# State products, context keys, values and set-up moved ahead at two stage joins of an eight-stage fp32 kernel, with six products of constants added

## The chip, the cores and the metric

The kernel runs on one core of a Trainium2 chip. The metric is the device time of the whole program in microseconds (us). The program is one launch, all data are fp32, and the host only transposes and regroups weights.

## The reference

Two sequences of 1024 rows of 256 columns (x, 2048 rows in all) go through eight residual stages. Each stage computes a layer norm of x, or works on x itself, and adds a gated result to x. They are lettered A to H. Two joins matter here: from E to F, and from F to G.

```python
def step(c, xt):                                   # stage F, a gated recurrence of two steps
    ft = sigmoid(xt @ wf.T + c @ uf.T + bf)
    it = sigmoid(xt @ wi.T + c @ ui.T + bi)
    gt = tanh(xt @ wc.T + c @ uc.T + bc)
    return ft * c + it * gt
h = tanh(x @ wo.T + c_final @ uo.T + bo)
# stage G: attention of 16 heads over 77 context rows, biased and masked
q = (LN(x) @ q_w.T + q_b); k = (ctx @ k_w.T + k_b); v = (ctx @ v_w.T + v_b)
attn = q k^T * scale + bias;  probs = masked softmax(attn)
x = x + tanh(g) * ((probs @ v) @ o_w.T + o_b)
```

In stage F the batch is the time axis: the two sequences are the two steps, and the first step starts from one given state c0, the same for every row. So the products of c0 with uf, ui and uc are constants of the run. In stage G the keys and values depend on the context alone and not on x.

## The kernel before

Each engine has its own instruction list, written out by hand stage after stage, and engines meet at counting semaphores. There is no planner: the order in each list is the order of the calls in the code. TensorE (PE) runs sim_pe (E), rnn_pe (F) and heads16_pe (G) in turn, VectorE (DVE) runs sim_dve, rnn_dve, norm_dve and heads16_dve, and ScalarE (ACT) has functions of the same names. x stays in SBUF as 16 tiles of 128 rows. Each finished tile has its statistics taken by finish (the update of x is L488, the statistics L490), and counts up the semaphore x_new. A matmul of the code is fp32 and appears as two instructions in the trace, so the counts in the rows are twice those of the code.

**Join E to F.** The last products of E are L1109. TensorE waits for all 16 tiles of E (x_new) and then makes the state products: three gates by two by two blocks with one moving column, L1308, into bank 7. VectorE waits for them, makes four small bias operations from them (L1424 to L1427), and only then norm_dve: seven small operations on the statistics (L656 to L662), a square root by ScalarE (L676), a reciprocal (L667). normed(0) then writes the first four normalised tiles (L1436), which TensorE transposes in two groups of two tiles (turn_x, L1323), each copied out by ScalarE (L1390). The gate products follow (from_x, L1330: 12 matmuls, 24 instructions, for each batch), ScalarE squashes them (L1397), and VectorE combines (gated, L1443 to L1452).

**Join F to G.** F has four steps s of two tiles and two batches. The last step ends with outputs(3) on TensorE (L1361 and L1368), summed(3) on VectorE (L1456, then L1459 twice), tanh by ScalarE (L1406) and update(3) on VectorE (L488 and L490 four times). TensorE waits for the last tile (x_new), then makes the context keys (L298, bank 4), the context values (values_ctx, L305, bank 7), turn_x(0) (L315) and queries(0) (L325). VectorE runs norm_dve, normed(0) (L505), then the set-up: four memsets of the value and count buffers and five small operations on the mask and one more memset (L510 to L521), then spread_k(0) (L526). It waits for the queries (take_q, L548), and goes on with spread_k(1), normed(1), shift(0, 0) (L565, L573, L574), spread_k(2), spread_k(3) and spread_v (L537 to L542). scores are L340, transposes of the weights L353, products with the values L367, projections L379.

```python
pe.wait_ge(sem("x_new"), NT + done("E", "x_new"))     # rnn_pe, ahead of the state products
...
dve.wait_ge(sem("F_u0_ps"), 1)                         # rnn_dve, ahead of the four bias operations
...
pe.wait_ge(sem("x_new"), NT + done("F", "x_new"))     # ahead of heads16_pe(pe, "G")
```

PSUM has eight banks. In F, bank 0 takes transposes and the last output products, banks 1 to 6 the gates of both batches, banks 7 and 6 the outputs. "ident" is the 128 x 128 identity, and "slots" a constant table, 512 columns wide; both are in SBUF from the start.

## Time and profile before

| what | value |
|---|---|
| median of 3 runs | 1467.87 us (1462.8, 1467.87, 1468.26) |
| profiled execution, its own time | 1465.94 us |
| its span, first to last instruction | 1464.1 us |
| TensorE busy | 1172.4 us, 80% |
| VectorE busy | 903.3 us, 62% |
| ScalarE busy | 523.9 us, 36% |
| GpSimd busy | 249.9 us, 17% |
| mean granted TensorE clock | 0.895 |

The clock is the share of full speed that TensorE was granted: 1.00 is 2.4 GHz and 0.50 is 1.2 GHz. The busy time of TensorE counts pipelined products from start to modelled end, so it overstates how full the engine is. The time outside the span is 1.84 us. The profiled execution lies between the lowest and the middle of the three runs.

### The profile page before, as it was taken

The numbers are of one execution on the slowest core, as the hardware profiler recorded it, in microseconds if no ns is written. First come the engines' busy times: TensorE is split into PE (matmuls) and PEld (weight loads), VectorE is DVE, ScalarE is ACT, GpSimd is POOL, SyncE is SP. The second block draws the span as 40 slices with busy tenths as digits, with TensorE's granted clock in tenths as the row PEclk, the third lists the DMA queues.
The fourth block names the chain that finished last, engine by engine and source line by source line (L and its number), as shares of the span: only waits on it lengthen the run. The fifth ranks groups of instructions, "written<-read, shape, count | busy, mean of one in ns | idle before, by whom it ended". The sixth has DMA issues, their size and how long they took to land.

```text
span 1464.1 us, 22555 instructions
## 1 busy us (share of the span) xinstructions
PE 1172.4 (80%) x8580; PEld 894.5 (61%) x8580; DVE 903.3 (62%) x2229; ACT 523.9 (36%) x1161; POOL 249.9 (17%) x220
## 2 busy tenths in 40 slices
PE   5988899995998898866999879898788963999500
PEld 4665688884456545653565768787566762888400
DVE  6889832348457646984645545255899975655333
ACT  3543434242347553531424211223244435434100
POOL 0009043300500000002010000000000002655376
PEclk9999989995899999997999879899799985999855
DMA  9200045400000003000000440000021002555443
GB/s 324 100 2 1 11 121 146 138 1 0 1 1 2 1 1 116 1 1 22 1 22 1 120 159 0 0 1 0 35 71 71 36 1 83 165 161 156 107 133 118
DMA packets 60001, 89.01 MB, mean 61 GB/s; under 512 B 21315, under 2 KB 50877, under 8 KB 57085
## 3 DMA queue, kind: packets, MB, share of 16 engines
q1 hardware_dynamic: 52413, 67.18, 14.1%
q0 software_dynamic: 7488, 20.46, 5.4%
q8 instruction: 68, 1.11, 0.3%
q14 instruction: 32, 0.26, 0.1%
HBM read 60.73 MB, written 26.89 MB: 60 GB/s over the span
## 4 chain that ended last, share of the span: by engine, by line
PE 53%; DVE 23%; issue 11%; ACT 6%; POOL 5%; DMA 1%; SPq 0%; POOLq 0%; DVEq 0%; ACTq 0%
PE ps L2454 5%; PE ps L1330 4%; POOL hall L2690 4%; PE ps L773 4%; PE ps L760 4%; PE ps L1836 3%; PE ps L2468 2%; DVE work L583 2%; PE ps L1850 2%; PE ps L367 2%; DVE work L574 2%; DVE work L573 2%; PE ps L1909 2%; PE ps L340 1%; DVE work L565 1%
## 5 line engine op out<-in xcount | busy, mean ns | idle before, releaser
L2679 POOL DMA_INDIRECT hall<-hall_rows,tile_idx x80 | 75.8, 948 | 423.2 <-DVE tile_idx L2597 376.4
L340 PE MATMUL ps<-hall,work 128*128 128x308 f32 x256 | 81.0, 442 | 12.1 <-DVE work L548 4.9
L1771 ACT ACTIVATE work<-ps,work 128x256 f32<-128x256 f32 x128 | 58.8, 472 | 84.7 <-DVE work L1659 84.6
L2454 PE MATMUL ps<-big,work 128*128 x320 | 84.4, 387 | 0.0
L367 PE MATMUL ps<-work,hall 78*32 78x128 f32 (+1 forms) x2048 | 69.7, 277 | 11.6 <-DVE work L584 8.5
L460 ACT COPY work<-ps 78x1024 f32<-78x1024 f32 (+1 forms) x64 | 64.3, 1004 | 40.4 <-PE ps L353 39.3
L367 PEld LDWEIGHTS ps<-work,hall 78*32 78x32 f32 (+1 forms) x2048 | 52.8, 110 | 36.5 <-ACT work L460 22.3
L353 PE MATMUL ps<-pack_const,work 128*78 128x128 f32 (+1 forms) x512 | 70.1, 281 | 3.0 <-issue 3.0
L583 DVE RECIPROCAL work<-ps 128x128 f32<-128x128 f32 x64 | 60.8, 951 | 13.7 <-PE ps L367 13.3
L2690 POOL DMA_INDIRECT hall<-expert_rows,back_idx x64 | 61.7, 964 | 39.4 <-DMA expert_rows<-work 20.2
L2652 DVE SCALAR_TENSOR_TENSOR x<-hall,work,x 128x256 f32<-128x256 f32 x64 | 31.2, 487 | 57.0 <-DMA hall<-expert_rows,back_idx 55.2
L1836 PE MATMUL ps<-big,dpack 128*128 128x384 f32 (+1 forms) x160 | 63.9, 563 | 1.9 <-ACT big L1748 1.0
L1330 PE MATMUL ps<-work,pack_F 128*128 128x256 f32 x288 | 64.8, 385 | 0.7 <-ACT work L1390 0.7
L353 PEld LDWEIGHTS ps<-pack_const,work 128*78 128x78 f32 (+1 forms) x512 | 56.1, 135 | 14.9 <-issue 11.5
L2601 DVE TENSOR_TENSOR work<-work,ps 128x128 f32<-128x128 f32 x80 | 23.2, 290 | 67.4 <-ACT work L2515 67.4
L340 PEld LDWEIGHTS ps<-hall,work 128*128 128x128 f32 x256 | 45.3, 197 | 25.3 <-DVE work L548 5.8
L1330 PEld LDWEIGHTS ps<-work,pack_F 128*128 128x128 f32 x288 | 55.5, 194 | 8.6 <-ACT work L1390 1.1
L760 PE MATMUL ps<-work,big 128*128 128x256 f32 x256 | 59.6, 393 | 0.7 <-ACT work L786 0.7
L2454 PEld LDWEIGHTS ps<-big,work 128*128 128x128 f32 x320 | 55.9, 195 | 4.6
L279 POOL TENSOR_TENSOR hall<-hall,mask_add 128x1232 f32<-128x1232 f32 x16 | 40.9, 2580 | 97.4 <-DMA hall<-in_fside 97.4
L773 PE MATMUL ps<-big,work 128*128 128x256 f32 x256 | 56.6, 379 | 0.0
L760 PEld LDWEIGHTS ps<-work,big 128*128 128x128 f32 x256 | 50.7, 199 | 8.4 <-ACT work L786 1.1
(497 smaller groups left out, 2695.2 us busy)
## 6 DMA issues: line engine op xcount, KB each, us to landing
expert_rows<-work SPq DMA_DIRECT2D x40, 256.0 KB, 2.2
masked_bias<-hall SPq DMA_DIRECT2D x8, 1232.0 KB, 5.2
dpack<-masked_bias SPq DMA_DIRECT2D x8, 1232.0 KB, 5.8
hall<-in_fside SPq DMA_DIRECT2D x8, 616.0 KB, 7.4
dpack<-in_pack_D SPq DMA_DIRECT2D x1, 4115.0 KB, 15.7
hall_rows<-hall SPq DMA_DIRECT2D x2, 2048.0 KB, 10.7
big<-in_w SPq DMA_DIRECT2D x4, 1024.0 KB, 11.1
big<-in_pack_B SPq DMA_DIRECT2D x1, 2052.0 KB, 10.1
```

Source lines behind the costliest of these rows:

```text
L340: mm = nc.tensor.matmul(o, A["qT"][:, c, b * P:(b + 1) * P], KV["kbd"][:, c, b, k * 4 * SC:(k + 1) * 4 * SC], start=True, stop=True)
L353: mm = nc.tensor.transpose(ps[0:SK[L], PT_BANK + h // 4, h % 4 * P:(h % 4 + 1) * P], weights_of(L, u)[:, h, :], ident)
L367: mm = nc.tensor.matmul(ps[j * HB32:(j + 1) * HB32, 4, half:half + P], lhsT, A["pT"][0:SK[L], u % 2, h * P:(h + 1) * P], start=g == 0, sto ...
L460: nc.scalar.copy(A["pT"][0:SK[L], u % 2, :].rearrange("p (k n) -> p k n", k=2), ps[0:SK[L], PT_BANK:PT_BANK + 2, :]).then_inc(s("pT_ready" ...
L583: link(ve.reciprocal(den, DEN_REG))
L760: mm = nc.tensor.matmul(ps[:, 1 + f // 2, f % 2 * D:(f % 2 + 1) * D], w["fc"][:, c * F0 + f * P:c * F0 + (f + 1) * P], BW["xnT"][:, c, :], ...
L773: mm = nc.tensor.matmul(ps[:, 5 + b, 0:D], BW["hT"][:, f, b * P:(b + 1) * P], w["proj"][:, f * D:(f + 1) * D], start=f == 0, stop=f == FC - 1)
L1330: mm = nc.tensor.matmul(ps[:, 1 + 3 * b + g, co * FJ * P:(co + 1) * FJ * P], w[kind + "fic"[g]][:, ci * D + co * P:ci * D + (co + 1) * P], ...
L1836: mm = nc.tensor.matmul(ps[:, bank, 0:n], w["wqkv"][:, ci * 3 * HDH + col:ci * 3 * HDH + col + P], LB["xnT"][:, ci, at:at + n], start=ci = ...
L2454: mm = nc.tensor.matmul(ps[:, GU_B[j % 2], 0:2 * INTER], MW["xT"][:, j % 2, c * P:(c + 1) * P], big[:, bass.ds(at + c * 2 * INTER, 2 * INT ...
L2679: gp.indirect_dma_start(out=FETCH_BUF[:, j % HT, :], out_offset=None, in_=hall_rows[:, :], in_offset=bass.IndirectOffsetOnAxis(ap=tile_idx ...
L2690: gp.indirect_dma_start(out=hall[:, t % NGB * TOP + k, :], out_offset=None, in_=expert_rows[:, :], in_offset=bass.IndirectOffsetOnAxis(ap= ...
```

## The change

What it does, and then the whole diff:

- The state products of F no longer wait for E's last tile. They go to bank 1 and are followed by two products of ident with slots (keep_busy(2, 2), into bank 2, which nobody reads before it is overwritten). VectorE makes its four bias operations after normed(0). TensorE waits for them once, ahead of the first gate product.
- The wait for F's last tile ahead of stage G is gone. The context keys come right behind the last output products. The values wait for the seventh increment of F_ysum_ready, the first L1459 of summed(3), which frees bank 7; four products of ident with slots (keep_busy(4, 5)) follow them, ahead of turn_x(0).
- G's set-up on VectorE becomes a function of its own and is called between gated(3, 1) and summed(3) in rnn_dve. Stage A makes the same set-up where it did. The wait for C_in moves with it.

```diff
--- before.py
+++ after.py
@@ -232,6 +232,11 @@
         block = ctx.enter_context(nc.Block())
 
 
+        def keep_busy(count, bank):
+
+            for _ in range(count):
+                nc.tensor.matmul(ps[:, bank, :], ident, pk["const"]["slots"], start=True, stop=True)
+
         UNITS = [(b, c) for b in range(B) for c in range(DC)]
         NU = len(UNITS)
 
@@ -381,7 +386,9 @@
                 mm.then_inc(s("y_ps"), 1)
 
             if L == "G":
+                pe.wait_ge(sem("F_ysum_ready"), (FS - 1) * FJ + 1)
                 values_ctx()
+                keep_busy(4, 5)
             turn_x(0)
             queries(0)
             if L == "A":
@@ -489,6 +496,22 @@
                                          op0=ALU.mult, op1=ALU.add))
             nc.vector.bn_stats(stats[:, t, :], x[:, t, :]).then_inc(done, 1)
 
+        def heads16_setup_dve(dve, L):
+            link, ve = chain_dve.link, nc.vector
+            link(ve.memset(KV["vpad"][0:SK[L]], 0.0))
+            link(ve.memset(KV["count"][0:SK[L]], 0.0))
+            for g in range(2):
+                link(ve.memset(KV["count"][0:SK[L], :, g, g * HD16:(g + 1) * HD16], 1.0))
+            if L == "G":
+                dve.wait_ge(sem("C_in"), LOADS["C"])
+                link(ve.tensor_copy(keep, mask8[:, :]))
+                link(ve.tensor_scalar(keep, keep, -1.0, 1.0, ALU.mult, ALU.add))
+                all_masked, counted = small[:, 4:4 + B], small[:, 8:8 + B]
+                link(ve.tensor_reduce(all_masked, mask_add[:, :, :], AX.X, ALU.max))
+                link(ve.tensor_scalar(all_masked, all_masked, 0.0, None, ALU.is_lt))
+                link(ve.tensor_tensor(counted[0:SC], keep, all_masked[0:SC], ALU.max))
+            link(ve.memset(small[:, 511:512], 0.0))
+
         def heads16_dve(dve, L):
             link = chain_dve.link
             w = pk[L]
@@ -496,8 +519,6 @@
             ve = nc.vector
             dve.wait_ge(sem("const_in"), 48)
             dve.wait_ge(sem(f"{L}_in"), LOADS[L])
-            if L == "G":
-                dve.wait_ge(sem("C_in"), LOADS["C"])
 
             def normed(n):
                 for b in range(B):
@@ -507,18 +528,8 @@
 
             normed(0)
             hm = pk["const"]["headmask"]
-            link(ve.memset(KV["vpad"][0:SK[L]], 0.0))
-            link(ve.memset(KV["count"][0:SK[L]], 0.0))
-            for g in range(2):
-                link(ve.memset(KV["count"][0:SK[L], :, g, g * HD16:(g + 1) * HD16], 1.0))
-            if L == "G":
-                link(ve.tensor_copy(keep, mask8[:, :]))
-                link(ve.tensor_scalar(keep, keep, -1.0, 1.0, ALU.mult, ALU.add))
-                all_masked, counted = small[:, 4:4 + B], small[:, 8:8 + B]
-                link(ve.tensor_reduce(all_masked, mask_add[:, :, :], AX.X, ALU.max))
-                link(ve.tensor_scalar(all_masked, all_masked, 0.0, None, ALU.is_lt))
-                link(ve.tensor_tensor(counted[0:SC], keep, all_masked[0:SC], ALU.max))
-            link(ve.memset(small[:, 511:512], 0.0))
+            if L == "A":
+                heads16_setup_dve(dve, "A")
             dve.wait_ge(s("kv_ps"), 1 + done(L, "kv_ps"))
 
             def spread_k(u):
@@ -539,7 +550,7 @@
                                               ALU.add))
                     if L == "G":
                         link(ve.tensor_scalar(KV["vpad"][0:SC, b], KV["vpad"][0:SC, b], keep[:, b:b + 1], None, ALU.mult))
-                        link(ve.tensor_scalar(KV["count"][0:SC, b], KV["count"][0:SC, b], counted[0:SC, b:b + 1], None, ALU.mult))
+                        link(ve.tensor_scalar(KV["count"][0:SC, b], KV["count"][0:SC, b], small[0:SC, 8 + b:9 + b], None, ALU.mult))
                 dve.sem_inc(s("kv_ready"), 1)
 
             def take_q(n):
@@ -1295,20 +1306,20 @@
         FS = HT // FJ
         GW = carve([("xn", (FJ, B, D)), ("xnT", (2, DC, B, FJ * P)), ("gate", (B, 3, DC * FJ * P)), ("c1", (DC, FJ * P)), ("c2", (DC, FJ * P)),
                     ("t", (FJ, D)), ("y", (FJ, B, D)), ("bias", (2, 3 * DC)), ("c0", (DC,))])
-        FY_BANK, FU_BANK = (7, 6), 0
+        FY_BANK, FU_BANK, FU0_BANK = (7, 6), 0, 1
 
         def rnn_pe(pe):
             w = pk["F"]
             pe.wait_ge(sem("F_in"), LOADS["F"])
 
-            pe.wait_ge(sem("x_new"), NT + done("E", "x_new"))
             for g in range(3):
                 for co in range(DC):
                     for ci in range(DC):
-                        mm = nc.tensor.matmul(ps[:, 7, g * DC + co:g * DC + co + 1],
+                        mm = nc.tensor.matmul(ps[:, FU0_BANK, g * DC + co:g * DC + co + 1],
                                               w["u" + "fic"[g]][:, ci * D + co * P:ci * D + (co + 1) * P],
                                               w["c0"][:, ci:ci + 1], start=ci == 0, stop=ci == DC - 1)
-            mm.then_inc(sem("F_u0_ps"), 1)
+            mm.then_inc(sem("F_u0"), 1)
+            keep_busy(2, 2)
 
             def turn_x(s):
                 for j in range(FJ):
@@ -1335,6 +1346,8 @@
 
             def from_x(s, b):
                 for g in range(3):
+                    if b == 0 and s == 0 and g == 0:
+                        pe.wait_ge(sem("F_u0"), 2)
                     if b == 0 and s:
                         pe.wait_ge(sem("F_gate_ready"), (s - 1) * 6 + g + 1)
                     if b and s:
@@ -1419,13 +1432,16 @@
             link, ve = chain_dve.link, nc.vector
             w = pk["F"]
             dve.wait_ge(sem("F_in"), LOADS["F"])
-            dve.wait_ge(sem("F_u0_ps"), 1)
-            b0, b1 = GW["bias"][:, 0, :], GW["bias"][:, 1, :]
-            link(ve.tensor_tensor(b0, ps[:, 7, 0:3 * DC], w["bias"], ALU.add))
-            link(ve.tensor_scalar(GW["bias"][:, 0, 0:2 * DC], GW["bias"][:, 0, 0:2 * DC], 0.5, None, ALU.mult))
-            link(ve.tensor_scalar(GW["bias"][:, 1, 0:2 * DC], w["bias"][:, 0:2 * DC], 0.5, None, ALU.mult))
-            link(ve.tensor_copy(GW["bias"][:, 1, 2 * DC:3 * DC], w["bias"][:, 2 * DC:3 * DC]))
             norm_dve(dve, "F")
+
+            def biases():
+                dve.wait_ge(sem("F_u0"), 1)
+                b0, b1 = GW["bias"][:, 0, :], GW["bias"][:, 1, :]
+                link(ve.tensor_tensor(b0, ps[:, FU0_BANK, 0:3 * DC], w["bias"], ALU.add))
+                link(ve.tensor_scalar(b0[:, 0:2 * DC], b0[:, 0:2 * DC], 0.5, None, ALU.mult))
+                link(ve.tensor_scalar(b1[:, 0:2 * DC], w["bias"][:, 0:2 * DC], 0.5, None, ALU.mult))
+                link(ve.tensor_copy(b1[:, 2 * DC:3 * DC], w["bias"][:, 2 * DC:3 * DC]))
+                dve.sem_inc(sem("F_u0"), 1)
 
             def normed(s):
                 if s:
@@ -1467,6 +1483,7 @@
                         finish(s * FJ + j + b * HT, GW["y"][:, j, b, :], None, 6, None, sem("x_new"))
 
             normed(0)
+            biases()
             normed(1)
             for s in range(FS):
                 gated(s, 0)
@@ -1476,6 +1493,7 @@
                         normed(s + 1)
                     update(s - 1)
                 gated(s, 1)
+            heads16_setup_dve(dve, "G")
             summed(FS - 1)
             update(FS - 1)
 
@@ -2798,7 +2816,6 @@
             heavy_pe(pe)
             sim_pe(pe)
             rnn_pe(pe)
-            pe.wait_ge(sem("x_new"), NT + done("F", "x_new"))
             heads16_pe(pe, "G")
             moe_pe(pe)
```

## Rows read from the trace of the kernel before

**Rows 1.** Page, the chain of work that ended last, by engine.

```profile
PE 53%; DVE 23%; issue 11%; ACT 6%; POOL 5%; DMA 1%; SPq 0%; POOLq 0%; DVEq 0%; ACTq 0%
```

**Rows 2.** Timeline, E to F: start, us, engine, line, op, operands, count, [idle before <-releaser].

```profile
913.33 1.03 PE L1109 MATMUL ps<-work,hall 128*128 128x256 f32 x4
...
915.37 0.43 DVE L490 BATCH_NORM_STATS2 stats<-x 128x6 f32<-128x256 f32 x1
...
915.95 4.54 PE L1308 MATMUL ps<-pack_F 128*128 128x1 f32 x24 [1.59 <-DVE stats L490]
...
921.43 0.19 DVE L656 TENSOR_TENSOR small<-stats 128x16 f32<-128x16 f32 x1
...
923.47 1.38 DVE L1436 TENSOR_SCALAR work<-x,mean,rstd 128x256 f32<-128x256 f32 x4
...
925.73 1.11 PE L1323 MATMUL ps<-pack_const,work 128*128 128x128 f32 x4 [0.68 <-ACT work L1390]
...
927.52 12.02 PE L1330 MATMUL ps<-work,pack_F 128*128 128x256 f32 x48 [0.68 <-ACT work L1390]
```

**Rows 3.** Busy time in stretches around E to F; columns: us, PE, PEld, DVE, ACT, POOL, PEclk, DMA.

```profile
916.70:920.50 3.80, 3.79 (x19) 3.70 (x18) 0.00 (x0) 0.00 (x0) 0.00 (x0) 0.50 0.00 0
...
927.50:930.40 2.90, 2.88 (x7) 2.35 (x8) 0.77 (x3) 1.27 (x1) 0.00 (x0) 0.50 0.00 0
930.40:941.00 10.60, 9.93 (x50) 8.56 (x49) 2.36 (x4) 3.10 (x7) 0.00 (x0) 1.00 0.00 0
941.00:1015.70 74.70, 73.29 (x347) 63.95 (x345) 36.27 (x69) 24.22 (x53) 0.00 (x0) 1.00 0.00 1
```

**Rows 4.** Timeline, F to G.

```profile
1016.02 1.99 PE L1368 MATMUL ps<-pack_F,work 128*128 128x256 f32 x8 [0.38 <-DVE work L1452]
1018.05 0.69 DVE L1456 TENSOR_TENSOR work<-ps,rows_F 128x512 f32<-128x512 f32 x1 [2.08 <-PE ps L1368]
1018.78 1.29 DVE L1459 TENSOR_TENSOR work<-ps,work 128x512 f32<-128x512 f32 x2
...
1023.70 2.42 PE L298 MATMUL ps<-ctxT,dpack 128*128 128x154 f32 x8 [5.69 <-DVE stats L490]
...
1025.72 0.73 DVE L505 TENSOR_SCALAR work<-x,mean,rstd 128x256 f32<-128x256 f32 x2
...
1026.61 0.91 DVE L510 MEMSET hall<- 77x1024 f32 x1 [0.16 <-issue]
...
1029.29 0.06 DVE L521 MEMSET small<- 128x1 f32 x1
1029.33 0.62 PE L315 MATMUL ps<-pack_const,work 128*128 128x128 f32 x4
...
1030.63 2.00 PE L325 MATMUL ps<-work,dpack 128*128 128x256 f32 x8 [0.68 <-ACT work L439]
1032.66 1.00 DVE L548 TENSOR_SCALAR work<-ps,dpack 128x256 f32<-128x256 f32 x2 [2.41 <-PE ps L325]
...
1046.76 3.42 PE L325 MATMUL ps<-work,dpack 128*128 128x256 f32 x8
```

**Rows 5.** Busy time in stretches from F into G.

```profile
1018.00:1022.50 4.50, 0.02 (x1) 0.00 (x0) 4.21 (x9) 2.51 (x3) 0.00 (x0) 1.00 0.00 0
...
1023.70:1029.30 5.60, 5.60 (x16) 4.22 (x17) 4.45 (x20) 0.21 (x1) 0.00 (x0) 0.50 0.00 0
...
1049.80:1190.00 140.20, 126.53 (x1557) 98.47 (x1555) 131.80 (x219) 56.95 (x70) 0.00 (x0) 1.00 0.16 56
```

**Rows 6.** Timeline, prices at full clock: one-column, 512-column, transposes, gate products.

```profile
863.35 1.05 PE L1127 MATMUL ps<-work 128*128 128x1 f32 x8 [1.18 <-DVE work L1275]
...
696.64 7.03 PE L2251 MATMUL ps<-dpack,big 128*128 128x512 f32 x16
...
963.14 0.66 PE L1323 MATMUL ps<-pack_const,work 128*128 128x128 f32 x4 [0.68 <-ACT work L1390]
963.63 10.53 PE L1330 MATMUL ps<-work,pack_F 128*128 128x256 f32 x48
```

## The prediction, on record before the changed kernel ran

> **What bounds the kernel now.** I read the page's chain first: TensorE holds 53% of it, VectorE 23% [rows 1]. That is an average over eight stages, so I went to the two joins that the change touches, with the timeline for the order of events and the stretches for what each engine and the granted clock did.
>
> At the join E to F the reader sees a queue of four things, one behind the other. E's last statistics end at 915.80. TensorE then makes 24 one-column products until 920.49, VectorE makes four bias operations, the norm starts at 921.43, and the first tiles are written from 923.47 [rows 2]. Only then come transposes and gate products, from 927.52. Behind them TensorE is busy 73.29 of 74.70 us at clock 1.00 [rows 3]: stage F is bound by TensorE, so what its first gate product gains, its last one gains too.
>
> At the join F to G the last tile releases the keys at 1023.70; keys and values run at clock 0.50, busy 5.60 of 5.60 us [rows 5], and the transposes of G start behind them at 1029.33. The normalised tiles had been ready since 1026.45, so TensorE is late and not VectorE. VectorE then waits 2.41 us for the queries [rows 4]. From there on it has work in a row, and in G's steady part it is busy 131.80 of 140.20 us [rows 5]: what the first queries gain, the end gains.
>
> **The sum for E to F.** The norm no longer stands behind products and biases: it starts 0.04 behind the statistics, at 915.84, not 921.43. That is 5.59 us. The tiles follow, the second at 923.47 + 0.69 - 5.59 = 918.57. What TensorE does until then:
> - State products start when E's products stop issuing, 913.33 + 4 x 0.217 = 914.2 (0.217 from 48 in 10.53, less 0.33 of the last, by 47 [rows 6]). One costs (1.05 - 0.25)/7 = 0.114 us at full clock [rows 6] (0.25 is one product's own length), so 24 cost 2.74, until 916.9.
> - Two constant products are four instructions of 512 columns. One costs (7.03 - 0.59)/15 = 0.43 [rows 6], so 1.7, until 918.65, 0.1 behind the second tile. At full clock they cost nothing, covered by the norm.
> - The bias operations (0.94 with their gaps, 920.49 to 921.43 before) lie behind normed(0), in VectorE's wait for the second transposes; the gate products need them some 2 us later. Nothing for them.
>
> Then the clock. In the trace before, TensorE stops with 256-column products at 914.36, makes one-column ones from 915.95, and the clock is 0.50 from 916.7. It stays there while the engine is busy 3.79 of 3.80 us with them, and comes back at 930.4 after 2.88 us of gate products [rows 3]. If the clock holds after the change, the transposes save 0.45 in the second group (1.11 to 0.66), some 0.2 in the first, and the 48 gate products 12.02 - 10.53 = 1.49 [rows 2, 6]: 5.6 + 2.1 = 7.7 us.
>
> If it falls, TensorE's list itself becomes long. At half clock a one-column product takes about 0.2 (19 of them in 3.80 us [rows 3]) and a constant 0.86 (twice 0.43). With the fall at 916.7 as before, two products are left (0.4) and the constants need up to 3.4, until 920.5, where the tile was ready at 918.6. The constants are wide, though, and 2.88 us of wide products brought the clock back before. I take it that it comes back at their end: transposes at 920.4, then 0.6 + 0.68 + 0.66 + 0.68, gate products at 922.9 and not 927.52, at full clock: 4.6 + 1.5 = 6.1. The bad end is a fall that the constants don't mend, say at 916.2: six products left (1.3), constants 3.4, until 920.9, then 1.1 + 0.68 + 1.1 + 0.68, gate products at 924.4, 3.1 early. I allow them twice the 2.9 us at half clock that they had before, which takes half of 2.9 back: 1.7.
>
> The weight load of a one-column product has a rule against the price I use. The Trainium skill, "TensorE: Matmul & The Clock Gate", section "LDWEIGHTS (loading the stationary operand)", gives columns / 1.2 GHz, 107 ns, whatever the granted clock; by it the six left at the bad end would cost 0.6 and not 1.3, and that end would be 2.4 and not 1.7. The trace disagrees: 0.114 apart at 1.00, 0.2 at 0.50, so 1.7 stands.
>
> **The sum for F to G.** The set-up moves ahead of summed(3). It takes 1029.35 - 1026.61 = 2.74, and VectorE has a wait of 2.08 there from 1015.97 [rows 4]. summed(3) starts at 1018.8 and not 1018.05, and everything behind it, tanh, updates and norm, is 0.8 later: a loss. Queued behind it are TensorE's values (bank 7), ScalarE's tanh and all of F's last updates. In return spread_k(0) follows normed(0) at once, which nobody waited for.
>
> TensorE: keys at 1017.9, 8 x 0.13 (0.217 for 256 columns, scaled to 154), then a wait for the first L1459, 1019.5 + 0.8 = 1020.3; values 8 x 0.217 until 1022.0; four constant products, eight instructions, 3.4, until 1025.4. The tiles of G come at 1026.1 + 0.8 and 1027.3. At full clock all of that is covered, with 1.5 us to spare, and the transposes end at 1027.8 and not 1029.95: 2.2 us. ScalarE's copy and the queries (2.00 [rows 4]) shift with them. But before, the queries already ran at full clock, which 5.6 us of keys and values had brought back; now a pause of 1.5 us, short transposes and a copy stand ahead of them. Should the clock fall there, the queries cost 3.42 (a later group at half clock, [rows 4]) and not 2.00, the transposes 0.4 more: 0.3 left, and the first scores at half clock take that too. Between 2.2 and about -0.3 I take 1.0, near the middle, as nothing in the rows says which.
>
> Sum: 6.1 + 1.0 = 7.1, call it 7.0. The profiled execution took 1465.94 (span 1464.1 and 1.84 around it), so it would become 1458.9. It is 1.9 below the median of the three runs, which lie 5.5 apart; from the median, 1467.87 - 7.0 = 1460.9. Neither join reads or writes DRAM; no DMA queue is moved past.
>
> **Rivals.**
> - *The clock holds at both joins.* 7.7 + 2.2 = 9.9: 1458.0. For it: all pauses left are 1.5 us or less, and in F's steady part pauses of 0.68 leave it at 1.00. Against: one-column products did not bring it back at full busy share. The Trainium skill, same page, section "The HAM clock gate (the 'warmup' mystery)", has the chip set the clock by how busy the engine has been recently; taken literally, 24 products in a row count as busy and this case is the one. The row of 916.7 to 920.5 speaks against it.
> - *The constants cost what they were to save.* The clock falls where they can't mend it and they run at half speed ahead of waiting tiles: 1.7 to 5 in F, middle 3.4, and 0 in G: 1464.5.
> - *Slower than before.* The clock falls right when E's products stop and again ahead of G's values. F: 24 x 0.2 + 3.4 puts the transposes at 922.6, gate products at 926.2, 1.3 early, with half clock for some 3 us more (1.5): 0.2 lost. G: values 3.5 and constants 6.9 at half clock end at 1030.7 and not 1029.33 (1.4), half-speed queries 1.4, scores 0.6: 3.4 lost. Together 3.6: 1471.5. It turns on whether the clock is at 0.50 by 1020; then the constants outlast their cover. It was 1.00 up to 1022.5 before [rows 5].
> - *No change*, because something else ends these joins: I find only the 0.8 on VectorE, which is in the sum.
>
> **How the numbers follow.** Forecast 0.42, clock held 0.24, costly constants 0.28, slower 0.06. A measurement of this kernel can tell about 0.5%, 7.3 us, from no change: the point 1460.5 lies inside the forecast. Faster by more gets the held clock and half the forecast, 0.45; slower by more than 0.5% needs the slower case's upper half, 0.03; the same, 0.52. The range reaches from a held clock with 2 us of scatter of the runs, 1456, to the costly case and 1 us more, 1465.5; the forecast's own is 1458.5 to 1463.
>
> **What would show it.** Right: VectorE's norm starts within 0.1 us of E's last statistics; state products 0.11 apart; TensorE's wait ahead of L1323 is gone or is for VectorE; summed(3) waits for nobody and starts about 0.8 late; values wait for L1459; turn_x(0) of G waits for VectorE. The granted clock between the state products and the first gates separates the cases: 1.00 throughout is the first rival, a short 0.50 the forecast, 0.50 into the gates the second. Wrong: constants over 0.5 us each at clock 1.00, transposes waiting for them by 2 us or more in both joins, or a gain at the gates that has gone by the end of F.

## The result, and the profile after

The changed kernel took 1454.0 us (median of 5 runs, 1452.24 to 1457.47); beside it the kernel before took 1467.87 (5 runs, 1462.8 to 1469.02). The ratio is 0.9916 [0.9893, 0.9939]. The forecast was 1460.9 with a range down to 1456.0: the sign was right, the size too small, and the measured time lies 2 us outside the range. By the ratio the gain is 12.3 us where 7.0 stood in the sum; the two traced executions lie 11.9 apart (1465.94 and 1454.0). A second comparison gave 0.9929 [0.9901, 0.9956], 10.4 us.

The page of the changed kernel, its engines and its chain of work that ended last:

```profile
PE 1168.9 (80%) x8592; PEld 889.8 (61%) x8592; DVE 896.6 (62%) x2229; ACT 524.5 (36%) x1161; POOL 250.8 (17%) x220
...
PE 52%; DVE 24%; issue 11%; ACT 6%; POOL 5%; DMA 1%; SPq 0%; POOLq 0%; DVEq 0%; ACTq 0%
```

Against [rows 1] the shares hardly move: 1 point from TensorE to VectorE. Such a page can't tell where 12 us went. The span fell from 1464.1 to 1452.2, and it has to be divided by stages. I measure a stage from the last statistics of the stage ahead of it to its own last statistics, or for H to the end of the span:

| | before | after | less |
|---|---|---|---|
| up to E's last statistics | 915.80 | 912.97 | 2.8 |
| stage F | 107.85 | 102.68 | 5.2 |
| stage G | 169.95 | 168.43 | 1.5 |
| stage H to the end | 270.50 | 268.10 | 2.4 |

The sum was made for F and G: 6.7 there, against 7.0. The other 5.2 lie where the forecast had no term: 2.8 ahead of the first changed instruction and 2.4 in H, in which no line was changed.

**E to F.** The timeline of the changed kernel, columns as in [rows 2], TensorE and VectorE:

```profile
911.36 2.81 PE L1318 MATMUL ps<-pack_F 128*128 128x1 f32 x24
912.54 0.43 DVE L497 BATCH_NORM_STATS2 stats<-x 128x6 f32<-128x256 f32 x1
913.00 0.19 DVE L667 TENSOR_TENSOR small<-stats 128x16 f32<-128x16 f32 x1
914.03 3.57 PE L238 MATMUL ps<-pack_const 128*128 128x512 f32 x4
915.04 1.38 DVE L1452 TENSOR_SCALAR work<-x,mean,rstd 128x256 f32<-128x256 f32 x4
917.44 0.60 PE L1334 MATMUL ps<-pack_const,work 128*128 128x128 f32 x4
918.72 0.66 PE L1334 MATMUL ps<-pack_const,work 128*128 128x128 f32 x4 [0.68 <-ACT work L1403]
920.05 10.63 PE L1341 MATMUL ps<-work,pack_F 128*128 128x256 f32 x48 [0.68 <-ACT work L1403]
```

And the same kernel's busy time in stretches, columns as in [rows 3]:

```profile
911.20:913.90 2.70, 2.70 (x26) 2.67 (x24) 2.10 (x8) 0.00 (x0) 0.00 (x0) 1.00 0.02 6
913.90:917.30 3.40, 3.40 (x6) 1.52 (x6) 2.71 (x12) 0.22 (x1) 0.00 (x0) 0.50 0.00 0
917.30:930.00 12.70, 11.35 (x55) 9.57 (x54) 3.73 (x8) 4.97 (x9) 0.00 (x0) 1.00 0.00 0
```

The norm begins 0.03 behind the statistics (912.97 to 913.00). The state products start (2.81 - 0.25) / 23 = 0.111 apart, where 0.25 is one product's own length. Then the granted clock is 0.50 from 913.9 to 917.3, almost exactly while the constants run; four of their instructions took 3.57 and not 1.7. The second tile was ready at 915.04 + 0.69 = 915.73, and the transposes began at 917.44, 1.7 later, behind the constants. From there on all is at full clock: transposes 0.60 and 0.66, 48 gate products in 10.63. Counted from E's last statistics the gate products begin at 7.09 (before 11.72) and end at 17.71 (before 23.74).

**F to G.** The changed kernel's timeline and stretches:

```profile
1010.05 0.69 DVE L1472 TENSOR_TENSOR work<-ps,rows_F 128x512 f32<-128x512 f32 x1
1010.78 1.29 DVE L1475 TENSOR_TENSOR work<-ps,work 128x512 f32<-128x512 f32 x2
1011.52 1.95 PE L310 MATMUL ps<-dpack,ctxT 128*77 128x256 f32 x8 [1.31 <-DVE work L1475]
1013.31 3.60 PE L238 MATMUL ps<-pack_const 128*128 128x512 f32 x8
1017.72 0.73 DVE L526 TENSOR_SCALAR work<-x,mean,rstd 128x256 f32<-128x256 f32 x2
1018.19 0.76 PE L320 MATMUL ps<-pack_const,work 128*128 128x128 f32 x4 [1.29 <-DVE work L526]
1019.63 3.68 PE L330 MATMUL ps<-work,dpack 128*128 128x256 f32 x8 [0.68 <-ACT work L446]
1023.35 1.00 DVE L559 TENSOR_SCALAR work<-ps,dpack 128x256 f32<-128x256 f32 x2 [4.12 <-PE ps L330]
```

```profile
1011.50:1019.70 8.20, 6.22 (x21) 3.10 (x21) 6.93 (x20) 3.42 (x6) 0.00 (x0) 1.00 0.00 0
1019.70:1023.10 3.40, 3.40 (x8) 2.40 (x8) 0.00 (x0) 1.18 (x1) 0.00 (x0) 0.50 0.00 0
```

Values wait for L1475 (L1459 before the change), and the constants are covered: transposes wait 1.29 for VectorE's tile. But the clock falls at 1019.70, just as the queries begin. They take 3.68, where [rows 4] has 2.00, and VectorE waits 4.12 for them, where it waited 2.41.

**G to H.** Sixteen-column products at the start of H. First the kernel before, timeline:

```profile
1195.83 2.73 PE L2404 MATMUL ps<-dpack,pack_F 128*128 128x16 f32 x16
```

and stretches:

```profile
1193.00:1196.60 3.60, 3.60 (x36) 3.60 (x34) 2.15 (x10) 1.74 (x3) 0.00 (x0) 1.00 0.00 0
1196.60:1244.30 47.70, 15.33 (x96) 10.82 (x96) 30.16 (x101) 22.81 (x43) 7.81 (x8) 0.50 0.20 64
```

Then the changed kernel, timeline:

```profile
1186.32 1.90 PE L2422 MATMUL ps<-dpack,pack_F 128*128 128x16 f32 x16
```

and stretches:

```profile
1184.00:1190.30 6.30, 4.22 (x39) 4.12 (x38) 3.57 (x27) 4.49 (x6) 0.00 (x0) 1.00 0.00 0
1190.30:1231.20 40.90, 10.62 (x77) 6.70 (x78) 27.84 (x82) 18.91 (x36) 5.93 (x6) 0.50 0.21 68
```

In both kernels the clock falls early in H and stays at 0.50 until the first experts. Before, it fell 3.0 us behind G's last statistics (1193.60) and came back 50.8 behind them; after, it fell 6.3 behind them (at 1184.08) and came back at 47.2. So 16 of these products took 1.90 and not 2.73. Take TensorE's products of H one by one, each counted from G's last statistics. Behind those sixteen the changed kernel is 0.83 ahead, and it is still 0.83 ahead at the experts' first products. At these two rows, a product that the experts make soon afterwards, it is 2.17 ahead (51.72 behind G's end before, 49.55 after), and 2.3 at the last product of H. TensorE's timeline before, then after:

```profile
1245.32 0.60 PE L2468 MATMUL ps<-big,work 128*128 x2
```

```profile
1233.63 0.60 PE L2486 MATMUL ps<-big,work 128*128 x2
```

So 0.8 of the 2.4 comes with the later fall, and 1.3 with the earlier return.

### The profile page after: what moved, and what is told of

Its sections match the earlier page's. It is cut to its first block, busy times and chain, and to the rows that moved or that the text cites. A ratio compares the mean times of both kernels' runs of the same rounds, so it can differ in the third digit from the quotient of the medians.

```text
span 1452.2 us, 22580 instructions
## 1 busy us (share of the span) xinstructions
PE 1168.9 (80%) x8592; PEld 889.8 (61%) x8592; DVE 896.6 (62%) x2229; ACT 524.5 (36%) x1161; POOL 250.8 (17%) x220
## 4 chain that ended last, share of the span: by engine, by line
PE 52%; DVE 24%; issue 11%; ACT 6%; POOL 5%; DMA 1%; SPq 0%; POOLq 0%; DVEq 0%; ACTq 0%
PE ps L2472 5%; PE ps L1341 4%; POOL hall L2708 4%; PE ps L771 4%; PE ps L784 4%; PE ps L1854 3%; DVE work L594 2%; PE ps L2486 2%; PE ps L1868 2%; PE ps L372 2%; DVE work L585 2%; DVE work L584 2%; PE ps L1927 2%; DVE work L576 2%; PE ps L345 1%
## 5 line engine op out<-in xcount | busy, mean ns | idle before, releaser
L358 PEld LDWEIGHTS ps<-pack_const,work 128*78 128x78 f32 (+1 forms) x512 | 55.7, 134 | 15.0 <-issue 11.9
```

The source lines that it names most:

```text
L358: mm = nc.tensor.transpose(ps[0:SK[L], PT_BANK + h // 4, h % 4 * P:(h % 4 + 1) * P], weights_of(L, u)[:, h, :], ident)
```

## The experiments

Theory T: the gain is the norm's at the join E to F, cut by a short fall of the clock; the F to G part is worth little; and the gain outside F and G is no effect of any single edit but of where in the work the clock changes. Rival R1: the F to G part and its constants carry a good share. Rival R2: constants are a cost. Rival R3: the clock at E to F is not set by what TensorE does in the join. All the kernels compute the whole output. The numbers of all the traces are in one table behind the last experiment; times there count from E's (or G's) last statistics. In groups of runs on one chip, the kernel before had the medians 1466.62 (the first four), 1464.69 (next four), 1471.89 (next four) and 1480.57 (last four).

**The changed kernel again, and each half alone.** No edit for the first:

> The changed kernel once more, nothing edited. In its first trace the two joins gave 6.7 us (E's last statistics to G's last ones), the stages ahead of the first changed instruction 2.8 and stage H 2.4. Theory J (joins): only the joins are the change's, the rest is what the granted clock happened to be in the stages outside; then the difference from the kernel before, over five more rounds, goes towards 7 (5 to 9) and the 2.8 and 2.4 are other numbers in this trace. Theory W (whole): the change makes the stages outside faster too; then it is again 11 to 14, and both come back within 0.5.

0.9929 [0.9901, 0.9956], median 1453.82. Behind E's last statistics the trace is the first one over again: gates at 7.09, F 102.69, H 268.08. Only E's end lies elsewhere, at 909.05 and not 912.97.

The E to F part alone (the set-up is back behind `normed(0)`, and F's `x_new` wait ahead of G's keys):

```
-                pe.wait_ge(sem("F_ysum_ready"), (FS - 1) * FJ + 1)
-                keep_busy(4, 5)
...
-            heads16_setup_dve(dve, "G")
...
+            pe.wait_ge(sem("x_new"), NT + done("F", "x_new"))
```

> The E to F join alone: state products early, biases behind the first tiles, the two constant products. G as before. J: 5.5 to 6.5 us at the join (statistics of E to the end of the first 48 gate products 17.7 and not 23.7), nothing at F to G, total 4 to 8 below before. W: the total is over 8 below. A rival to both, that F's gain is lost by the end of F: statistics of E to those of F stay at 107.8.

0.9944 [0.9922, 0.9966]. In the trace E to the end is 539.63, 8.7 less than before, and the whole change has 539.14 in the trace of the same group. G's queries end 110.41 behind E's end, with the whole change 110.34; G ends at 271.10 against 271.06. Its queries are at full clock. The half clock has moved back to keys and values, with the queries bound as before:

```profile
1013.19 2.42 PE L303 MATMUL ps<-ctxT,dpack 128*128 128x154 f32 x8 [5.69 <-DVE stats L495]
...
1019.71 2.00 PE L330 MATMUL ps<-work,dpack 128*128 128x256 f32 x8 [0.67 <-ACT work L444]
```

The F to G part alone (E's `x_new` wait back ahead of the state products, biases ahead of the norm, no constants there):

```
+            pe.wait_ge(sem("x_new"), NT + done("E", "x_new"))
...
-            keep_busy(2, 2)
...
+            biases()
             norm_dve(dve, "F")
```

> The F to G join alone: keys, values and set-up early, the four constant products. F as before. J: summed(3) 0.8 late, first queries ready 1 to 2 us earlier if the clock holds up to them, 0 if it falls; total 0 to 3 below before, which five rounds hardly tell from none. W: 4 or more below.

0.9988 [0.9968, 1.0008]: nothing that can be told. In the trace G ends 277.49 behind E, before 277.80. In this trace the clock came back late in F's first gate products (17.96 behind E's end, before 14.57). Beside the traces of the kernel before in which it did so too (277.91 to 278.20), the part is worth 0.4 to 0.7. So R1 falls by the traces; the times alone allow this part up to 0.3%. The E to F part carries the change, but with its two constants, as the next runs show.

**Without constants.** All six out, two out at F, four out at G:

```
-            keep_busy(2, 2)
...
-                keep_busy(4, 5)
```

> The changed kernel without its six constant products, all else moved as it was. If they hold or bring back the clock, as the forecast had it, the gate products of F's first step begin at clock 0.50 (48 in 12 us and more, not 10.6) and G's queries take 3.4 us and not 2.0: 2 to 4 us slower than the changed kernel. Rival: they only fill, and without them TensorE is free earlier at both joins: the same or up to 1 us faster.

> The changed kernel without the two constant products of the E to F join; the four of F to G stay. Theory A (alignment): the clock falls and returns at the same places of the program's own progress in every run (0.92 us behind E's last statistics in five traces of six, 0.90 in the other), so joins repeat to 0.1 us, and constants act where they lie. It expects F as in the kernel without any constants: gate products start 6.1 behind E's last statistics, the 48 take 13.1, so 1.5 slower than the changed kernel at this join. Theory L (luck): where the clock falls is drawn anew in each run; then the join scatters by 1 us or more between traces of equal code.

> The changed kernel without the four constant products of the F to G join; the two of E to F stay. A: F again 102.7 long, gate products as in the changed kernel (start 7.1, 48 in 10.6); the clock falls before the queries, which take 3.4 to 3.8 and end 8 to 8.4 behind F's last statistics, where the changed kernel has 7.66: these constants are worth 0.4 to 0.8 only. H is then 268.1 or 270.1, by where the clock falls at its start. L: none of these repeats.

The ratios are 0.9978 [0.996, 0.9997], 0.9949 [0.9927, 0.9971] and 0.995 [0.9933, 0.9968]. What the two constants at F do is seen in TensorE's timeline without them (the second of these kernels):

```profile
912.03 2.81 PE L1318 MATMUL ps<-pack_F 128*128 128x1 f32 x24
916.17 1.12 PE L1333 MATMUL ps<-pack_const,work 128*128 128x128 f32 x4 [1.34 <-DVE work L1451]
917.97 1.12 PE L1333 MATMUL ps<-pack_const,work 128*128 128x128 f32 x4 [0.68 <-ACT work L1402]
919.76 13.10 PE L1340 MATMUL ps<-work,pack_F 128*128 128x256 f32 x48 [0.68 <-ACT work L1402]
```

Transposes no longer stand behind anything, and the gate products begin 0.97 earlier, at 6.12 behind E's end. But everything is at half clock until 11.16, and the gate products end at 19.21 and not 17.71: two constants are worth 1.5 at F's first gates. By G's end that had gone where the four at G were in (270.96 without the two, 271.06 with them), and had grown to 3.2 where the four were out (274.30 without the two, 271.14 with them); there the queries were again at half clock (3.78 and not 1.99). The four at G are worth 0.2 at the queries with the two at F in (110.54 without, 110.34 with). With the two out they are worth 2.15 there (112.30 and 110.15) and 3.3 by G's end. These are single traces.

The times say more. In one group the changed kernel had 0.9929 and the kernel without any constants 0.9978, and the two intervals don't touch. By the ratios some 7 of the 10 us hang on the six constants; in the traces it is 5.2 of 9.1 behind E's end (544.37 and 539.14). So R2 falls, and the moves without constants are worth only some 3 to 4 us. No run has the constants without the moves.

**The set-up back in its old place:**

```
-            heads16_setup_dve(dve, "G")
             summed(FS - 1)
...
-            if L == "A":
-                heads16_setup_dve(dve, "A")
+            heads16_setup_dve(dve, L)
```

> The changed kernel with G's set-up back behind normed(0), its old place. The forecast's term: the early set-up delays F's end by 0.8 and buys nothing, as VectorE only waits for the queries. So F is 101.9 long and not 102.7, and the queries start 3.2 behind... the same distance behind F's last statistics less nothing: end of queries 0.8 earlier if the clock is the same. Rival: spread_k(0) ready late (3 us of set-up behind the tiles) holds the first scores, and the gain is given back.

0.9951 [0.9925, 0.9977], against 0.9929 and 0.9916 for the whole change; the intervals overlap. F is 101.84 and not 102.68: the 0.84 that the early set-up costs, as forecast. G's end has 270.79 against 271.06: only 0.3 of it is kept. The queries had ended 1.62 earlier (108.72 and 110.34), so most of that was lost inside G; the set-up stood ahead of spread_k(0) again, and whether that is the reason was not tried. What was gained by then H took: 270.87 against 268.08, with its sixteen logit products in 2.64.

**The constants divided.** If the clock falls because of the narrow state products, one wide product ahead of them and one behind should hold it (R3: they change nothing):

```
+            keep_busy(1, 2)
             for g in range(3):
...
-            keep_busy(2, 2)
+            keep_busy(1, 2)
```

> The changed kernel with its two constants of E to F apart: one directly behind E's last products, ahead of the state products, the other behind these. In all traces the clock fell while the one-column state products ran. A: wide work ahead of them keeps it at 1.00, the transposes no longer wait for slow constants, and gate products start 5.2 to 5.8 behind E's last statistics and not 7.1, the 48 in 10.5: 1.5 to 2 faster at this join; what G and H do then depends on where their falls come, plus or minus 2. Rival: one wide product changes nothing, the clock falls at 0.92 as before, and the join is within 0.3 of the changed kernel.

0.9917 [0.9888, 0.9946], in a group where the kernel before has a median of 1464.69; its own median, 1451.25, is the lowest of the first eight. Timeline and stretches:

```profile
907.28 1.02 PE L238 MATMUL ps<-pack_const 128*128 128x512 f32 x2
908.14 2.73 PE L1319 MATMUL ps<-pack_F 128*128 128x1 f32 x24
910.74 1.10 PE L238 MATMUL ps<-pack_const 128*128 128x512 f32 x2
911.68 0.60 PE L1335 MATMUL ps<-pack_const,work 128*128 128x128 f32 x4
914.29 10.63 PE L1342 MATMUL ps<-work,pack_F 128*128 128x256 f32 x48 [0.68 <-ACT work L1404]
```

```profile
907.00:911.00 4.00, 4.00 (x30) 3.47 (x29) 2.88 (x12) 0.22 (x1) 0.00 (x0) 1.00 0.00 0
911.00:914.30 3.30, 1.95 (x11) 0.94 (x10) 2.58 (x10) 1.22 (x3) 0.00 (x0) 1.00 0.02 5
```

The clock never falls at this join. Gates begin at 5.40 and end at 16.03, F takes 101.00, the queries 1.99, and E to the end is 536.15: 3.1 less than the changed kernel and 12.1 less than before. In the four other traces of kernels with this edit the gates again start at 5.39 or 5.40. The ratio alone does not tell this kernel from the changed one (0.9916 and 0.9929), so the 3.1 are a reading of the traces. R3 falls: what TensorE does in the join matters. It is not all that matters, as a later trace of the changed kernel's join shows.

**Is H's share the clock's return?** In the traces so far H was 268.08 to 268.53 where the clock came back 47.2 or 47.3 behind G's end and 269.86 to 270.87 where it came back after 50.6 to 51.1. I tried to move the return alone, by three wide constants ahead of the first experts, in the divided kernel, in that kernel with the late set-up, and in the kernel before; with them the kernel before again:

```
+            keep_busy(3, 2)

             def turn_rows(j):
```

> The kernel before once more, nothing edited, for a second trace of it. Theory A (alignment): the stages ahead of E's end differ by some us from trace to trace with equal code (908.9 to 917.4 in ten traces), but behind E's end the traces repeat: 548.3 us from E's last statistics to the end, F 107.85, H 270.5, the last 16 logit products in 2.7. Where the return of the clock is a near thing, as in the F-to-G-alone kernel (48 gate products 13.7 and not 12.0 with the same code ahead of them), F can be 109.5. Theory L (luck): the stretch behind E scatters by 3 us or more, as the one ahead of it does.

> The kernel with the two constants of E to F apart, and three more constant products in stage H, in the 5.5 us in which TensorE waits for the first rows of the experts (bank 2). The clock is 0.50 there and the first expert's products run at it. If a price of H is the clock at the experts' start, they start at 1.00: four of L2454's products in 1.03 and not 1.92, H 1 to 2 shorter than 268.5, and E's last statistics to the end 534 to 535.5 and not 536.15. If H's start is bound by the rows' DMA or by the other engines, H stays within 0.3.

> The same with G's set-up back behind normed(0). The early set-up delayed F by 0.84; late, the tiles of G come 0.84 earlier, and if the clock still holds at the join, the queries end at 106.1 behind E's last statistics and not 106.97. H moves with the place of its first fall: 268 or 270. Expected E to end 533 to 536; more than in the kernel with the set-up early would mean that alignment of H is worth more than the set-up's place.

> The kernel before with only the three constants of stage H. It tells what the clock at the experts' start is worth without any change at the joins: H 268.5 to 269.5 and not 270.5, if it is worth what the changed kernel's trace suggests (1.3 of its 2.4); the 0.8 of the logit products, at the stage's start, stay.

The ratios: the kernel before against itself 0.9998 [0.998, 1.0016], then 0.9936 [0.9917, 0.9955], 0.9918 [0.9896, 0.994] and 0.9992 [0.9976, 1.0009]. The clock did return at 43.6 to 44.0 in all three with the edit. H did not shorten: 275.36 to 275.73 with it, 275.54 without. In this group even the unchanged kernel had an H 5 us longer than in its first trace, and right behind the return stood a pause of all engines. Its row in the unchanged kernel's timeline, ScalarE:

```profile
1252.29 0.37 ACT L2511 COPY work<-ps 128x256 f32<-128x256 f32 x1 [5.08 <-remote]
```

The other engines stood still for a shorter time at this place: VectorE 2.98, TensorE 3.52, GpSimd 2.21. Up to the pause the trial can be read. In the kernel before with the edit the clock returned 6.8 earlier (43.57 and not 50.41 behind G's end), and the same product as above started 1.9 earlier, at 49.19 and not 51.10. Without the edit, then with it, TensorE:

```profile
1246.84 0.60 PE L2468 MATMUL ps<-big,work 128*128 x2
```

```profile
1241.16 0.60 PE L2475 MATMUL ps<-big,work 128*128 x2
```

Behind the pause nothing of it was left (H 275.41 and 275.54). What the return is worth by H's end can't be read from this trial, so I ran it again, with the whole change in it and with the divided kernel with and without the edit (the last has the late set-up too):

> The kernel before with three constant products in stage H ahead of the first expert, as in the earlier run, whose session had a stall of some 5 us on all engines right behind that place and hid what came of it. Theory A (alignment): the changed kernel's H was 2.4 shorter only because the clock fell 3.4 later at its start (logit products 1.90 and not 2.73) and came back 3.6 earlier at the experts (47.2 and not 50.8 behind G's last statistics). Then constants that bring it back at 43.6 to 47.4 make H of the kernel before 268 to 269 and not 270.5, without any change at the joins. If H stays at 270.1 to 270.9, the place of that return is worth nothing and the 2.4 have another cause. A session with the stall (H about 275.5) decides nothing.

> The changed kernel with the same three products in H. Its clock already came back at 47.2, so by theory A there is little left: H 267 to 268.1, and E's last statistics to the end 538.2 to 539.2 (539.2 without them). If these products are worth as much here as in the kernel before, alignment is not what they mend.

> Constants of E to F apart, and the three of H, once more for a session without the stall: E's last statistics to the end 534.5 to 536.2 (536.15 without the three). Against the changed kernel: 3 to 4.5 faster.

> Constants of E to F apart, G's set-up back in its old place, nothing in H. From the two earlier kernels with it late: F 100.14, queries end 106.11 behind E's last statistics (106.97 with it early), G's last statistics at 267.4 and not 267.64: of 0.86 only 0.2 arrives, as the set-up then stands ahead of spread_k(0). So the total is within 0.5 of the kernel with the two apart, and H between 268 and 270.9 by alignment.

Against 1480.57: 1.0004 [0.9987, 1.0022], 0.9889 [0.9862, 0.9916], 0.9862 [0.9839, 0.9885], 0.9876 [0.9854, 0.9898]. The pause was there again in every H (275.6 to 277.0). With the edit H was 275.63, without it 277.03, 1.4 apart, for two kernels that differ in the set-up too. At the product named above the edit had only 0.35 of that, with the return 3.6 earlier; the rest arose in the pause or behind it. So the return moves the experts' start, as seen three times, and what reaches H's end without a pause is shown only by the first pair of traces. The rows of the two show how the edit works, first with it, then without:

```profile
1217.22 5.46 PE L238 MATMUL ps<-pack_const 128*128 128x512 f32 x6
1224.07 1.03 PE L2475 MATMUL ps<-big,work 128*128 x4
```

```profile
1225.80 1.92 PE L2471 MATMUL ps<-big,work 128*128 x4
```

In this group the timed gains over the kernel before (16 to 22 us) are 11 to 13 us more than the traces show behind E (4.0, 10.6 and 9.4). Most of that is the trace they are compared with. It is of the kernel before with the three constants, and caught its quickest execution, 1471.98 us, 8.6 below the median of the kernel before; and 3 to 5 us lie ahead of E's end (916.09 against 912.89, 911.25 and 913.00). No trace shows what makes most executions there some 9 us longer than this one. Within the group times and traces agree: 1463.89 against 1458.22 is 5.7, the traces have 6.6.

The run of the whole change in it was the most telling. In the join E to F it is the changed kernel, instruction for instruction, yet the clock fell 0.62 behind E's last statistics and not 0.91. TensorE's timeline and the stretch:

```profile
911.29 3.07 PE L1318 MATMUL ps<-pack_F 128*128 128x1 f32 x24
914.22 3.76 PE L238 MATMUL ps<-pack_const 128*128 128x512 f32 x4
917.77 1.06 PE L1334 MATMUL ps<-pack_const,work 128*128 128x128 f32 x4
...
921.30 10.92 PE L1341 MATMUL ps<-work,pack_F 128*128 128x256 f32 x36 [0.67 <-ACT work L1403]
```

```profile
913.50:927.10 13.60, 12.25 (x31) 8.11 (x31) 4.35 (x18) 3.51 (x6) 0.00 (x0) 0.50 0.00 0
```

The constants did not bring it back. It came back 14.27 behind E's end, with the gate products under way, which started at 8.41 and took 13.51. F was 106.89: of the changed kernel's F gain 4.2 us gone. That is the rival of the costly constants, as it was written, and the division of the constants (101.00 in the same group) avoids it.

**All traces.** "Gates" is the start and length of the first 48 gate products; "fall, return" are the granted clock's, behind E's end around the join E to F ("none": it stays at 1.00), and behind G's end in H.

| kernel | gates | fall, return | F | queries | G ends | H: fall, return | H |
|---|---|---|---|---|---|---|---|
| before | 11.72 + 12.02 | 0.92, 14.57 | 107.85 | 2.00 | 277.80 | 3.0, 50.8 | 270.50 |
| after | 7.09 + 10.63 | 0.91, 4.33 | 102.68 | 3.68 | 271.12 | 6.3, 47.2 | 268.10 |
| after, again | 7.09 + 10.63 | as after | 102.69 | 3.68 | 271.06 | 6.3, 47.3 | 268.08 |
| E to F part alone | 7.09 + 10.63 | as after | 101.84 | 2.00 | 271.10 | 6.3, 47.3 | 268.53 |
| F to G part alone | 11.73 + 13.69 | 0.90, 17.96 | 110.39 | 1.99 | 277.49 | 3.3, 51.1 | 270.12 |
| no constants | 6.12 + 13.10 | 0.92, 11.16 | 104.19 | 3.78 | 274.30 | 3.1, 50.9 | 270.06 |
| none at F | 6.12 + 13.10 | 0.92, 11.16 | 104.19 | 1.99 | 270.96 | 3.0, 50.8 | 270.75 |
| none at G | 7.09 + 10.63 | as after | 102.68 | 3.52 | 271.14 | 6.3, 50.6 | 269.86 |
| set-up late | 7.09 + 10.63 | as after | 101.84 | 2.91 | 270.79 | 3.2, 51.0 | 270.87 |
| divided | 5.40 + 10.63 | none | 101.00 | 1.99 | 267.64 | 6.3, 47.3 | 268.50 |
| before, third group | 11.91 + 13.51 | 0.72, 17.78 | 109.54 | 1.99 | 277.98 | 6.0, 50.4 | 275.54 |
| before + 3 in H, third group | 11.99 + 13.43 | 0.63, 17.69 | 109.54 | 1.99 | 277.91 | 6.0, 43.6 | 275.41 |
| divided + 3 in H, third group | 5.40 + 10.63 | none | 101.00 | 1.99 | 267.54 | 6.2, 43.8 | 275.36 |
| divided, late + 3 in H | 5.39 + 10.63 | none | 100.14 | 1.99 | 267.36 | 6.4, 43.9 | 275.73 |
| before + 3 in H, fourth group | 11.78 + 13.65 | 0.86, 17.93 | 109.55 | 1.99 | 278.20 | 6.0, 43.5 | 275.68 |
| after + 3 in H | 8.41 + 13.51 | 0.62, 14.27 | 106.89 | 1.99 | 273.97 | 3.1, 44.1 | 275.90 |
| divided + 3 in H | 5.40 + 10.63 | none | 101.00 | 1.99 | 267.64 | 6.1, 43.7 | 275.63 |
| divided, late | 5.39 + 10.63 | none | 100.15 | 1.99 | 267.44 | 6.3, 47.2 | 277.03 |

## Why the prediction was right, and where it was not

**Right: the join E to F.** Forecast were the norm 0.04 behind the statistics, state products 0.114 apart, a fall of the clock behind E's wide products, constants at half speed ahead of a ready tile, the return with their end, and gates 4.6 earlier and 1.5 shorter. Measured were 0.03, 0.111, the fall 0.91 behind the statistics, 3.57 us of constants, a return 0.15 ahead of the transposes, and 4.63 earlier and 1.4 shorter: 6.0 of 6.1. The bank and the wait for the biases cost nothing, as said. Both other cases of this join exist, too. The held clock was priced 1.6 above the forecast, and the divided constants gave 1.7 more in F. The costly constants came up in one of the six traces of kernels whose code is the changed kernel's up to the end of this join.

The Trainium skill, "TensorE: Matmul & The Clock Gate", section "The HAM clock gate (the 'warmup' mystery)", has the clock follow how busy the engine has been. The trace does not agree if a row of one-column products counts as busy: TensorE was busy 2.70 of 2.70 us up to the fall. With one of the two constants moved ahead of the same 24 it held, in five traces of five.

**Right in total, wrong in its parts: F to G.** 1.0 was taken between 2.2 and -0.3; the runs show 0.0 at G's end (271.12 with the part, 271.10 without). The loss of 0.8 by the earlier set-up came to 0.84. "Should the clock fall there, the queries cost 3.42 and not 2.00" came true with 3.68, and ate the rest: the low end was the case, and I took the middle for want of a row. The E to F part was worth 6.7 by G's end (6.0 by F's): its queries ended 0.4 sooner behind F's end, the clock there being back at 4.90 behind F's end and not 5.71, and the other 0.3 came later in G. That the clock is the reason was not tried. So F and G together gave 6.7 for 7.0, by luck in the second term.

**Wrong: the step "what the first queries gain, the end gains".** It let the sum end with G and priced stage H at nothing, without a row for it. Stage H, in which nothing changed, was 2.4 shorter, as the clock fell 6.3 and not 3.0 behind G's last statistics and was back 3.6 earlier. The rows of before that I chose have nothing of H; one stretch behind G's end would have shown 47.70 us at 0.50, that is, a stage whose length hangs on where two changes of the clock fall. It was to be in the range, some 2 us to either side. The step fails inside G too: with the set-up late the first queries ended 1.62 earlier and G only 0.3. H's share goes with where the clock changes, not with any one edit: with the set-up late, or no constants at F, G ends no later and H is 2.7 us longer (270.79 and 270.87, 270.96 and 270.75).

**Wrong: the range took one trace of before for the kernel before.** Ahead of the first changed instruction the two traces are 2.8 apart, and why stays open; over all the traces here E's end, on unchanged code, lies between 908.89 and 918.65. And the trace that I read had the kernel before at its better alignment: F 107.85, while three other traces of it, or of it with an edit in H only, have 109.54 or 109.55, the clock coming back 3.2 us later into the gate products. Against those the change gains 6.9 in F and not 5.2. But that sets the worse case of one kernel beside the better one of the other. The one pair in which both have the later return, in the last group, gives 109.55 and 106.89, 2.7 in F and 4.0 behind E. Scatter of 2 us was allowed only beyond one rival, where a sum of 7.0 needed several us on both sides. With 9.1 behind E in the traces (11.2 by the means in the second comparison), I take 9 to 12 us for the true size of the change. That last is an argument from the spread, not a run; the last group lies on either side of it, with 4.0 in its traces and 16 to 17 in its times.

## What to carry to other kernels

An engine with work in a row can lose its clock to narrow work: look at the granted clock around each join, and where a run of narrow products stands between wide ones, put wide ones on both sides and not only behind. Of constants that are to keep a clock, one ahead and one behind did what two behind did not: 1.7 us more in the first stage, and repeatably. When an edit shifts a join by some us, price also the next stages that run at the lower clock, even if nothing in them is touched, and give them a range of both signs. A trace is of one execution: before setting traces against times, see where the traced execution lies among the timed ones.

## What the runs showed of the hardware

- The clock fell from 1.00 to 0.50 with TensorE busy in 2.70 of 2.70 us (24 one-column products in it), and in H of the kernel before with 3.60 of 3.60 (sixteen-column products and 128 x 128 transposes in turn). One-column products start 0.111 apart at 1.00; in the kernel before 19 took 3.80 at 0.50, 0.2 each.
- A few tenths of a us decide, or less. The same code in the same join had the fall 0.91 behind E's end and F 102.68, or at 0.62 and F 106.89. The join of the kernel before had it at 0.92 and the return at 14.57, or at 0.63 to 0.90 and the return at 17.69 to 17.96 (four traces). Within each case the traces repeat each other within 0.02 us (F 102.68, 102.69, 102.68; with the divided constants 101.00 three times).
- Transposes of fp32 tiles follow the clock: four took 0.60 at 1.00 and 1.12 at 0.50; 512-column products start 0.43 apart at 1.00, and 0.85 at 0.50 (0.99 between the first two of a row).
- In the last two of the four groups every trace had a pause 51 to 60 us into H, whose cause the traces don't show: ScalarE idle for 3.3 to 5.1 us, TensorE for 2.3 to 3.5, GpSimd for 1.5 to 2.4. H was 275.4 to 277.0 there and 268.1 to 270.9 in the others.
